# A causal attention kernel: the mask of the diagonal block moves from TensorE's products to additions of VectorE in PSUM

## What is computed

```python
x = x + _layernorm(attn(_layernorm(x)))        # the part spoken of here
x = x + _layernorm(ffn(_layernorm(x)))         # untouched

q = (x @ wq.T + bq).reshape(B, S, H, hd)       # k and v alike; B=2, S=2048, H=16, hd=64
scores = jnp.einsum('bqhd,bkhd->bhqk', q, k) * inv_sqrt_hd
causal = jnp.triu(jnp.ones((S, S), dtype=bool), k=1)
scores = jnp.where(causal[None, None, :, :], -jnp.inf, scores)
probs = jax.nn.softmax(scores, axis=-1)
attn = jnp.einsum('bhqk,bkhd->bqhd', probs, v).reshape(B, S, D)
return attn @ wo.T + bo
```

## Time and profile before

| what | us |
|---|---|
| three runs | 2646.74, 2645.48, 2641.49 |
| their median | 2645.48 |
| the profiled execution, from outside | 2647.44 |
| its span, first to last instruction | 2645.3 |
| first projections and normalization | 0 to about 125 |
| steps 0 to 2 of pair 0, alone | 125 to 142 |
| pairs 0 to 14 with their projections | 142 to 2026 |
| pair 15 | 2026 to 2166 |
| finish phase | 2166 to 2645 |

### The profile page before, as it was taken

How to read it: one execution, slowest core, us unless ns; L and a number is a source line. 1 busy time by engine, 2 the same in 40 slices (tenths; PEclk the granted TensorE clock), 3 DMA queues, 4 the chain that set the end, 5 groups by cost and what they waited for, 6 DMA issues and landing times. The chain is left out here.

```text
span 2645.3 us, 73670 instructions
## 1 busy us (share of the span) xinstructions
PE 2369.8 (90%) x29650; PEld 1509.0 (57%) x29650; DVE 1704.6 (64%) x3706; ACT 1711.6 (65%) x2451; POOL 1829.9 (69%) x1551
## 2 busy tenths in 40 slices
PE   3789999999999997989999999999998559999995
PEld 2447576656656655656665757575765335444543
DVE  6466667666766654556656656666565446888887
ACT  2277777767767765667767777777777653444443
POOL 2278888878878776768878777887887653555553
PEclk9999999999999998999999999999999669999997
DMA  7499999999999999999999999999999985666663
GB/s 201 102 162 180 194 187 205 189 187 184 198 178 185 182 183 181 190 175 176 173 168 180 168 156 170 179 164 182 167 166 184 172 167 118 153 153 154 150 159 88
DMA packets 1433794, 450.33 MB, mean 170 GB/s; under 512 B 1410256, under 2 KB 1411680, under 8 KB 1433456
## 3 DMA queue, kind: packets, MB, share of 16 engines
q1 hardware_dynamic: 1433456, 445.63, 91.8%
HBM read 68.01 MB, written 41.94 MB: 42 GB/s over the span
## 5 line engine op out<-in xcount | busy, mean ns | idle before, releaser
L790 POOL TENSOR_TENSOR hl<-probs,hl 128x1024 f16<-128x1024 f32 (+7 forms) x768 | 1229.3, 1612 | 426.3 <-ACT hl L671 424.8
L514 DVE TENSOR_REDUCE neg_max<-s_ps 128x1 f32<-128x1024 f32 (+7 forms) x768 | 696.3, 907 | 449.1 <-PE s_ps L380 377.6
L665 ACT ACTIVATE probs<-s_ps,exp_bias 128x1024 f32<-128x1024 f32 (+7 forms) x768 | 655.5, 854 | 448.3 <-DVE exp_bias L517 444.2
L671 ACT ACTIVATE hl<-probs 128x1024 f16<-128x1024 f32 (+7 forms) x768 | 620.5, 808 | 58.6 <-DMA pt<-hl 34.8
L398 PE MATMUL o_ps<-v,pt 128*128 128x65 f16 x4352 | 452.7, 194 | 92.0 <-DMA pt<-hl 84.4
L374 PE MATMUL s_ps<-nat 64*128 64x512 f16 (+3 forms) x3840 | 441.9, 360 | 63.4 <-ACT probs L665 61.4
L398 PEld LDWEIGHTS o_ps<-v,pt 128*128 128x128 f16 x4352 | 404.2, 97 | 142.1 <-DMA pt<-hl 69.4
L399 PE MATMUL o_ps<-v,pt 128*128 128x65 f16 x4352 | 452.7, 195 | 0.0
L400 PE MATMUL o_ps<-v,pt 128*128 128x65 f16 x4352 | 450.9, 193 | 0.0
L427 PE MATMUL u_ps<-arena,w 128*128 128x512 f16 x992 | 386.5, 390 | 54.4 <-DMA arena<-hl 41.5
L399 PEld LDWEIGHTS o_ps<-v,pt 128*128 128x128 f16 x4352 | 404.0, 98 | 26.7 <-issue 0.6
(11 more groups left out here) (149 smaller groups left out, 3757.6 us busy)
## 6 DMA issues: line engine op xcount, KB each, us to landing
w_raw<-in_w_pairs SPq DMA_DIRECT2D x48, 576.0 KB, 4.7
o_scratch<-o_hl SPq DMA_DIRECT2D x128, 128.0 KB, 3.6
out<-result SPq DMA_DIRECT2D x32, 512.0 KB, 3.6
x_in<-in_x SPq DMA_DIRECT2D x27, 512.0 KB, 4.6
pt<-hl SPq DMA_TRANSPOSE x768, 4.5
probs<-in_x SPq DMA_DIRECT2D x16, 512.0 KB, 4.6
xn_scratch<-xn SPq DMA_DIRECT2D x16, 512.0 KB, 3.9
xn<-in_x SPq DMA_DIRECT2D x11, 512.0 KB, 3.8
```

The costliest lines, as they stand in the source:

```text
L514: nc.vector.tensor_reduce(neg_max[:, r, acc, h:h + 1], s_ps[n % S_RING][:, 0:nb * P], AX_X, ALU.max, negate=True).then_inc(max_done, 1)
L665: nc.scalar.activation(probs[n % P_RING][:, 0:nb * P], s_ps[n % S_RING][:, 0:nb * P], ACT.Exp, bias=exp_bias[:, r, acc, h:h + 1], scale=SO ...
L671: nc.scalar.activation(hl[n % HL_RING][:, 0:nb * P], probs[n % P_RING][:, 0:nb * P], ACT.Copy).then_inc(p_hi_done, 1)
L790: nc.gpsimd.tensor_tensor(hl[n % HL_RING][:, w:2 * w], probs[n % P_RING][:, 0:w], hi, ALU.subtract).then_inc(p_lo_done, 1)
```

## The change

The four products of L380 go. In `row_max` two additions of VectorE take their place, one a head: the last 128 columns of `s_ps` plus `mask`, in place in PSUM, where `mask` is now one fp32 tile in SBUF with all 128 columns. Both additions stand ahead of the first maximum of the step, and each maximum waits for the addition of its own head (`mask_done`). One constant is loaded in place of two, and the wait for constants moves from TensorE's start to VectorE's first `row_max`.

```diff
@@ scores (TensorE) @@
                 for at in range(0, nb * P, 512):
                     end = min(nb * P, at + 512)
                     keys = slice(k0 * P + at, k0 * P + end)
-                    diagonal = end == nb * P and k0 + nb == t + 1
                     for q, k in ((q_lo, k_hi), (q_hi, k_lo), (q_hi, k_hi)):
                         for h in range(2):
                             mm = nc.tensor.matmul(s_ps[(n + h) % S_RING][:, at:end], qk[HEADS[h], q, rows],
-                                                  qk[HEADS[h], k, keys], start=(q == q_lo),
-                                                  stop=(q == q_hi and k == k_hi and not diagonal))
-                    if diagonal:
-                        for part in range(2):
-                            for h in range(2):
-                                mm = nc.tensor.matmul(s_ps[(n + h) % S_RING][:, end - P:end], unit_rows[HEADS[h], part, :],
-                                                      mask[HEADS[h], part, :], start=False, stop=(part == 1))
+                                                  qk[HEADS[h], k, keys], start=(q == q_lo), stop=(q == q_hi and k == k_hi))
                 mm.then_inc(s_done, 2)
...
-            pe.wait_ge(consts_loaded, 48)
...
@@ row_max (VectorE) @@
                 r, (t, k0, nb, acc) = i // PER_ROUND, STEPS[i]
+                diagonal = k0 + nb == t + 1
+                masked = 2 * (QT * p + sum(k0 + nb == t + 1 for t, k0, nb, acc in STEPS[:i]))
+                dve.wait_ge(s_done, NTASK * p + 2 * i + 2)
+                if diagonal:
+                    for h in range(2):
+                        last = s_ps[(NTASK * p + 2 * i + h) % S_RING][:, (nb - 1) * P:nb * P]
+                        nc.vector.tensor_tensor(last, last, mask[:], ALU.add).then_inc(mask_done, 1)
                 for h in range(2):
                     n = NTASK * p + 2 * i + h
-                    dve.wait_ge(s_done, NTASK * p + 2 * i + 2)
+                    if diagonal:
+                        dve.wait_ge(mask_done, masked + h + 1)
                     nc.vector.tensor_reduce(neg_max[:, r, acc, h:h + 1], s_ps[n % S_RING][:, 0:nb * P], AX_X, ALU.max,
                                             negate=True).then_inc(max_done, 1)
...
             split_weight(1, "k")
+            dve.wait_ge(consts_loaded, 32)
             for i in range(LAG):
                 row_max(0, i)
```

More of the change, by code:

```diff
@@ L10 @@
 F16 = mybir.dt.float16
-BF16 = mybir.dt.bfloat16
 AX_X = mybir.AxisListType.X
@@ L106, in units_ending, with attend_phase @@
     return [i // STEPS_PER_UNIT] if UNITS[kind] and i >= 0 and i % STEPS_PER_UNIT == STEPS_PER_UNIT - 1 else []
-def attend_phase(nc, x, w_pairs, unit_in, mask_in, xn_scratch, o_scratch, arena, fin):
+def attend_phase(nc, x, w_pairs, mask_in, xn_scratch, o_scratch, arena, fin):
     with ExitStack() as ctx:
@@ L138, in attend_phase @@
         o_hl = sb("o_hl", [P, 2, 2, 4, 2 * HD], F16)
-        unit_rows = sb("unit_rows", [P, 2, P], BF16)
-        mask = sb("mask", [P, 2, P], BF16)
+        mask = sb("mask", [P, P], F32)
         x_in, xn = fin["x_raw"], fin["x_pair"]
@@ L181, in attend_phase @@
         s_done = sem("s_done")
+        mask_done = sem("mask_done")
         max_done = sem("max_done")
@@ L340, in _ @@
             sp.dma_start(fin["ident"][:], fin["ident_in"]).then_inc(consts_loaded, 16)
-            sp.dma_start(unit_rows[:], unit_in).then_inc(consts_loaded, 16)
             sp.dma_start(mask[:], mask_in).then_inc(consts_loaded, 16)
@@ L1405, in _, with attention_ffn @@
             steps(step)
-def attention_ffn(nc, x, w_pairs, w_o, b_o, ffn_in, ffn_probe, ffn_mix, center, slope, ident, unit_rows, mask, own,
+def attention_ffn(nc, x, w_pairs, w_o, b_o, ffn_in, ffn_probe, ffn_mix, center, slope, ident, mask, own,
                   rank, out):
@@ L1413, in attention_ffn @@
         fin = finish_inputs(nc, ctx, x, o_scratch, w_o, b_o, ident, ffn_in, ffn_probe, ffn_mix, own, rank, center, slope)
-        attend_phase(nc, x, w_pairs, unit_rows, mask, xn_scratch, o_scratch, fin["arena"], fin)
+        attend_phase(nc, x, w_pairs, mask, xn_scratch, o_scratch, fin["arena"], fin)
         finish_phase(nc, fin, out)
@@ L1420 @@
            L0_ffn_lora_degen, L0_ffn_bias_w, L0_ffn_debias_w):
-    import ml_dtypes
     import numpy as np
@@ L1439 @@
                              np.arange(N_EXP)])
-    by_half = lambda m: np.tile(m.reshape(2, HD, P).transpose(1, 0, 2), (2, 1, 1)).astype(ml_dtypes.bfloat16)
     arrays = {
@@ L1453 @@
         "ident": np.eye(P, dtype=np.float32),
-        "unit_rows": by_half(np.eye(P)),
-        "mask": by_half(np.where(np.arange(P)[None, :] > np.arange(P)[:, None], -1e30, 0.0)),
+        "mask": np.where(np.arange(P)[None, :] > np.arange(P)[:, None], -1e30, 0.0).astype(np.float32),
         "own": (np.arange(2 * N_EXP)[:, None] == expert[None, :]).astype(np.float32),
```

## The result

The changed kernel takes 2619.19 us (median of 7 runs, 2612.73 to 2622.45), the kernel before, beside it on the same chip, 2645.48 us (7 runs, 2632.34 to 2654.97). The ratio is 0.9911, with a 95% interval of 0.9891 to 0.9931: faster by 26 us, where I had forecast 2644 in a range from 2629 to 2660. The profiled execution has a span of 2617.4 us. Every experiment's runs stand beside runs of the kernel before on the same chip, whose medians lay between 2640.4 and 2645.6.

What follows compares the result with a forecast made beforehand. TensorE's own work was taken to bound pairs 0 to 14, with pair 15 a chain of waits. Terms -16.5 + 6.6 + 1 + 4 + 0.7 + 1.2 = -3.0 us gave 2644 us, range 2629 to 2660.

Steps and rivals of the forecast that it cites:

- Not all of it can be kept: Of 26 us on offer, TensorE's gain before step 6's second head becomes a longer DMA wait; -16.5 us remain.
- The price of a step's products: Without its mask products, each diagonal step gives TensorE back 0.11 us, the projection starting earlier.
- Five steps swallowed in the DMA stretch: Gains in steps 2, 4, 5, 7 and 8, plus one for step 18, are lost; 10 of 16 count.
- GpSimd blocking: Rival: additions contend with GpSimd, waits up to 2 us in many steps; +77, over 2700 us; chance 3%.
- Step 14: Its scores wait for step 13's exponential, delayed by additions: 0.51 us each, 13 such waits, +6.6 us.
- What the additions cost in sum: Added delays: step 14 6.6, step 6 1, pairs 0 to 6 4, start 0.7, pair 15 1.2 us.
- the +4 for pairs 0 to 6: VectorE also normalizes the second sequence there; eight more tight steps at 0.5 us, ends 0 and 8.
- the +1 for the thin cover of step 6: Step 4's delay reaches step 6's scores; the DMA wait hides it except in four pairs, +0.25 us each.
- Pairs 0 to 7 unchanged: Pairs 0 to 6 were to stay about unchanged in length, pairs 8 to 14 each up to 1 us shorter.
- Pair 15: About five of 13 exponential waits have a diagonal maximum on the chain: +1.2 us, at most 7.
- margins cover: Rival: additions fit VectorE's idle time everywhere; -14.5 us, about 2631, down to 2622; chance 28%.
- The loop through VectorE: Rival: scores, maximum, exponential, next scores becomes the limit at scores 2, 3, 6, 14; 2658 to 2668 us; chance 22%.

Runs made afterwards that it cites:

- e5: The change with TensorE's mask products in steps 2, 4, 5, 7 and 8 of every pair, additions in the other eleven diagonal steps; 2639.07 us, 0.9981.
- e1: The change with the mask left out altogether, neither TensorE's products nor VectorE's additions; 2613.99 us, 0.9871.
- e8: The change with both additions made twice in every diagonal step, the second waiting for the first; 2624.94 us, 0.9943.
- e13: The change with 64 small products (128 instructions) put ahead of TensorE's first projection; 2647.57 us, 1.0027.
- e15: The change with 32 small products (64 instructions) put ahead of TensorE's first projection; 2640.29 us, 1.0003.
- e14: The change with mask products in step 13 of each pair (2640.02 us), plus 84 small products (168 instructions) ahead of the first projection; 2623.75 us, 0.9932.
- e11: The change with mask products in pairs 8 to 15 and additions in pairs 0 to 7; 2637.44 us, 0.9979.
- e9: The kernel before, all products kept, with the four output stores issued three steps later, in steps 5 and 17; 2620.72 us, 0.9922.

## Why the prediction was wrong, step by step

- **The step that failed** is in "Not all of it can be kept": that TensorE's gain up to 1451.74 "becomes a longer wait" for the transposes. It took the landing of the transposes as given by SyncE's queue. It was not: waits for transposes in pairs 8 to 14 went from 20.9 to 7.4 us, and the half clock from 17.1 to 3.4. At step 6 an instruction packet started in the transpose's flight in pairs 9, 11 and 13 before, and in none after; at step 18 one does in every pair 9 to 13 in both kernels, but sooner behind the issue after, and the transposes take 5.3 to 5.9 us instead of 5.9 to 6.5. No term of my sum and no rival had a change in DMA durations from outside the kernel's own transfers. That one effect is about 20 us (13.5 of waits and 6.9 of clock); the sum without it, -3.0, stands against about -5 with the place averaged. That these two agree is partly luck, since the products gave more than I kept of them and the additions probably took less.
- **The price of a step's products** was right: the projection starts 0.06 us before the last score product's end, and the score segments of pairs 8 to 14 are 13.8 us shorter over 112 steps, 0.12 each.
- **Five steps swallowed in the DMA stretch** (and one at step 18) was wrong: products in these five steps alone (e5) are not free, they cost 20 us, though most of that is the place. In the trace of pairs 8 to 14 the products' time arrives for all 16 steps.
- **The additions' duration**: 0.29 us predicted, 290 ns median. The overlap was larger than I took: the second starts 0.21 us after the first, and the maximum 0.41 after the first (median of 256), where I had 0.45. By the Trainium skill, VectorE: DVE Perf Modes, section "The DRAIN you can't avoid", a next operation that is not held starts earlier than when the pipeline is empty; I had taken from there only its first rule, with the full 0.58 us. The measured 0.21 us agree with the former.
- **GpSimd blocking**: none; the additions take 272 to 300 ns over 512 cases. The row of L541 was the right one to read.
- **Step 14**: predicted 0.51 us a pair later behind `times_v`; in pair 10 it is 0.50 (its scores start 0.78 us after the start of the last product of `times_v`, 1466.58 to 1467.36, where it was 0.28 in the earlier trace rows). Waits for exponentials before 2041 us: 20.4 to 31.5, predicted up by 5 to 10. Mechanism and place right.
- **What the additions cost in sum**: I had 6.6 + 1 + 4 + 0.7 + 1.2 = 13.5 us. Leaving them out (e1) gives back 5 (11 by the ratios), doubling them costs 6 to 8, and beside the products they cost 0 (-5 to +5). The term was probably twice too large, but the intervals don't exclude it. Step 14's wait is real, but part of such a delay may only stand in for another wait: with the additions doubled (e8), waits for exponentials from 142 to 2041 us rise from 31.5 to 49.0, and those for transposes fall from 73.0 to 59.6. No run separates the +4 for pairs 0 to 6 and the +1 for the thin cover of step 6, so both stay unshown.
- **Pairs 0 to 7 unchanged**: right (1033.0 to 1034.0), but not by my reason. The products' 14 us or so are there given back as waits for transposes (41.3 to 50.0), waits for exponentials (13.8 to 18.8) and half clock (48.8 to 55.3, of which half is lost). The place matters there too: 1041.2 us in e13, 1027.6 in e15. Whether the additions or the place do it at offset 0 was not taken apart.
- **Pair 15** a little longer: wrong, 141.2 to 136.0. In the other profiles it is 137 to 143 with or without products, so these 5 us are no finding.
- **Small misreadings in the working**: the gap between dependent VectorE operations is 0.04 us by its own row (1470.85 to 1470.89), not 0.03; the DMA share of 1.04 is that of all transfers, not of the transposes alone; and step 14's 0.40 us was not derived from the 0.45 above it. None of the three moves the sum by more than 1 us.
- **The rivals**: "margins cover" named 2631 and, for more, 2622, with the right sign, yet its reason (no growth in the waits for exponentials) did not come true. The loop through VectorE did not take over: TensorE's waits for exponentials before pair 15 grew by 11 us, under the 20 that I had set as its sign, and VectorE had room for 512 more additions (e8).

Open is how an instruction packet holds up a transpose inside the DMA engines. It was shown that its start in the flight goes with a later landing, and that moving TensorE's instructions against the packets moves the time of the kernel; not by what mechanism.

## What to carry to other kernels

In a repeating loop whose DMA engines are busy nearly all the time (a share of 0.98 to 1.06 in pairs 8 to 14 here), the number of instructions in the loop, and of those ahead of it, sets where the instruction packets fall. That alone moved this kernel by 28 us (1.1%). Before an edit that adds or removes instructions is credited or blamed, shift the offset by a quarter, a half and three quarters of a packet with idle instructions and take the mean. What helped at every place tried was to take the fragile spot away: here stores that stood ahead of transposes which TensorE waits for.

## What the runs showed of the hardware that I had not expected

- TensorE's instructions come in 16 KB packets by DMA while the kernel runs, one for every 256 instructions (13 a pair for 3332), each some 1 us long in the records. The profile counts them on the same 16 DMA engines as the kernel's transfers (0.6% of their time).
- The second transpose of step 6, with such a packet starting in its flight, takes 4.6 to 6.4 us (mean 5.82 of 26), without one mostly 4.4 (mean 4.42 of 54).
- 128 small instructions in an idle stretch at the start, with nothing else touched, cost 28 us of 2619 (e13), and 168 of them gained some 15 (e14).
- In pairs 8 to 14 of the kernel before, each of the five stretches at the lower of the two clock levels starts 0.4 to 1.6 us after TensorE took up work again from a wait of 1.7 to 2.8 us for a transpose. Such a stretch does not follow every wait: over pairs 8 to 14 of all 20 profiles, 9 of 30 waits of 2 us or more for a transpose have none behind them, one of 3.2 us in e11 among them. The lower level takes 17.1 us before, 3.4 after (behind a wait of 2.0 us for an exponential), 20.5 in e13, and nothing in e9. In e13 it is 8.5 of the 29.4 us.
